# Three pairs of gate and up sums ahead of the first products: re-ordering the opening of a fused FFN-attention-FFN kernel on one core

## The reference

```
x = x + 0.5 * ffn(layernorm(x))
x = x + attn(layernorm(x))          # chunked gated linear attention, 4 heads
x = x + 0.5 * ffn(layernorm(x))

ffn(x): scores = softmax(x @ gate_w.T); keep the 8 best of 64, w_e
        flat = w_e[:, inv_map]                      # 8 groups of 8
        scalar = flat.sum(-1); soft = softmax(where(flat == 0, -1e9, flat))
        xg = x + soft @ mask_up_w                   # one per group
        g = xg @ gate_proj_w.T; u = xg @ up_proj_w.T    # 352 inner columns per group
        y = sum over groups of scalar * (silu(g) * u) @ down_proj_w.T
```

## Time and profile before

| | |
|---|---|
| median of 3 timed runs | 1857.75 us (1857.65 to 1857.84) |
| the profiled execution's own time | 1859.35 us |
| its span in the profile | 1857.6 us |
| TensorE busy | 1837.3 us (99%), 8608 matmuls |
| VectorE, ScalarE, GpSimd busy | 841.1, 525.6, 140.5 us (45%, 28%, 8%) |
| DMA | 366.83 MB, mean 197 GB/s |
| mean granted TensorE clock | 0.999 |

### The profile page before, as it was taken

One profiled execution on the slowest core, in us unless ns is written; L12 is line 12 of the kernel. 1 busy time (PEld: TensorE's weight loads), 2 busy tenths in 40 slices (PEclk: granted clock), 3 DMA queues, 4 the chain that ended last, 5 costly groups with the idle time before them and its releaser, 6 DMA issues.

```text
span 1857.6 us, 22348 instructions
## 1 busy us (share of the span) xinstructions
PE 1837.3 (99%) x8608; PEld 1529.7 (82%) x8608; DVE 841.1 (45%) x1599; ACT 525.6 (28%) x802; POOL 140.5 (8%) x246
## 2 busy tenths in 40 slices
PE   7999999999999999999999999999999999999999
PEld 5888888888888888888888888888888888888887
DVE  7557453555345563324433556344654324422222
ACT  3324322532124432112212533124532111311111
POOL 1131110100000000000010010000100000000000
PEclk9999999999999999999999999999999999999999
DMA  5986755445455455476655555455455466657664
GB/s 193 384 304 241 265 189 179 161 171 173 148 193 183 160 171 177 134 260 213 224 183 183 177 193 171 160 192 177 156 170 175 146 223 217 210 174 241 220 238 170
DMA packets 90345, 366.83 MB, mean 197 GB/s; under 512 B 11680, under 2 KB 12064, under 8 KB 69504
## 3 DMA queue, kind: packets, MB, share of 16 engines
q1 hardware_dynamic: 50064, 262.89, 40.3%
q10 hardware_dynamic: 27792, 47.20, 9.3%
q0 software_dynamic: 12384, 55.32, 7.7%
HBM read 323.55 MB, written 41.81 MB: 197 GB/s over the span
## 4 chain that ended last, share of the span: by engine, by line
PE 94%; DVE 3%; ACT 1%; issue 1%; DMA 0%; SPq 0%; ACTq 0%; DVEq 0%
PE bank L1057 27%; PE bank L1059 27%; PE bank L1058 27%; PE bank L1270 4%; PE bank L1067 1%; PE bank L1211 1%; PE bank L1203 1%; PE bank L1210 1%; PE bank L1197 1%; PE bank L1255 1%; PE bank L1256 0%; PE bank L1087 0%; PE bank L1088 0%; PE bank L1095 0%; DVE act_t L677 0%
## 5 line engine op out<-in xcount | busy, mean ns | idle before, releaser
L1057 PE MATMUL bank<-x_hi,wt 128*128 128x512 f32 x1328 | 524.0, 395 | 0.0
L1059 PE MATMUL bank<-x_lo,wt 128*128 128x512 f32 x1328 | 517.8, 390 | 0.0
L1058 PE MATMUL bank<-x_hi,wt 128*128 128x512 f32 x1328 | 517.0, 389 | 0.0
L677 DVE TENSOR_TENSOR act_t<-bank,sig 128x512 f32<-128x512 f32 x176 | 121.6, 691 | 568.9 <-PE bank L1270 511.7
L1059 PEld LDWEIGHTS bank<-x_lo,wt 128*128 128x128 f32 x1328 | 249.2, 188 | 53.2
L1058 PEld LDWEIGHTS bank<-x_hi,wt 128*128 128x128 f32 x1328 | 249.6, 188 | 50.2
L1057 PEld LDWEIGHTS bank<-x_hi,wt 128*128 128x128 f32 x1328 | 249.5, 188 | 49.5
L1057 PE MATMUL bank<-dt,a_hi 128*128 128x512 f32 x704 | 279.1, 396 | 0.3 <-DVE a_lo L677 0.3
L1059 PE MATMUL bank<-dt,a_hi 128*128 128x512 f32 x704 | 274.8, 390 | 0.0
L1058 PE MATMUL bank<-dt,a_lo 128*128 128x512 f32 x704 | 274.4, 390 | 0.0
L601 ACT ACTIVATE sig<-bank 128x512 f32<-128x512 f32 x176 | 105.5, 599 | 526.7 <-PE bank L1270 526.6
(11 more groups left out here) (178 smaller groups left out, 1684.0 us busy)
## 6 DMA issues: line engine op xcount, KB each, us to landing
wt<-scr_w SPq DMA_DIRECT2D x140, 1152.0 KB, 5.2
dt<-scr_d SPq DMA_DIRECT2D x140, 512.0 KB, 5.2
s_bc<-scr_s ACTq DMA_DIRECT2D x128, 256.0 KB, 5.1
state<-wat POOLq DMA_DIRECT2D x28, 512.0 KB, 6.4
scr_w<-wt POOLq DMA_DIRECT2D x12, 1024.0 KB, 7.9
b_all<-wgu SPq DMA_DIRECT2D x22, 512.0 KB, 7.9
scr_d<-dt POOLq DMA_DIRECT2D x22, 512.0 KB, 4.0
scr_w<-tw POOLq DMA_DIRECT2D x10, 1024.0 KB, 7.7
```

The costliest lines, as they stand in the source:

```text
L677: return nc.vector.tensor_tensor(dst, a, b, op)
L1057: mm(dst, wh, xh, start=start, stop=False)
L1058: mm(dst, wl, xh, start=False, stop=False)
L1059: return mm(dst, wh, xl, start=False, stop=stop)
```

## The change

GpSimd takes over the remainders of chunk 2 (`gu_lo(2)`), and ScalarE rounds chunk 2 ahead of five small DMA issues. Chunk 2's gate and up sums go to `YB[2]` and `YB[3]` and are computed before the `soft` products of chunk 0: the gate sums between the transposes of `scal` and `route`, the up sums behind those of `route`. The two transposed routing halves go to `W1` and `W0` instead. In the loop the gate sums of chunk 3 come with n = 2 and its up sums with n = 3, `masked(2)` and `masked(3)` stand in n = 1 and 2, and `down(0)`, `masked(4)`, `down(1)` come behind chunk 3's sums, `down(2)` and `down(3)` in n = 4. From n = 5 on the order is the old one. ScalarE's `m_top`, VectorE's `m_mask` and `m_rest` of chunks 3 and 4 move one chunk earlier, with n = 1 and n = 2; `gu_hi(4)` and `gu_lo(4)` stand in n = 2 ahead of the rest of it, and the decay weights move from n = 1 to n = 2.

```diff
         def g_bank(n):
-            return YB[0] if n == 1 else GB
+            return YB[2 * n - 2] if n in (1, 2) else GB
         def u_bank(n):
-            return YB[1] if n == 1 else UB
+            return YB[2 * n - 1] if n in (1, 2) else UB
...
+            def gu_lo(c):
+                pool.wait_ge(gu_hi_ok, c + 1)
+                w = first_w(c)
+                nc.gpsimd.tensor_tensor(w[:, GW:2 * GW], raw_gu[:, c % 2, :], w[:, 0:GW].bitcast(F32),
+                                        ALU.subtract).then_inc(gu_lo_ok, 1)
...
                 if c + 1 < CH:
                     store_w(c + 1)
+                if c == 0:
+                    gu_lo(2)
                 store_m(c)
...
             m_top(0)
+            gu_hi(2)
             act.dma_start(raw_k1, w_gk1).then_inc(ld_const, 16)
...
-            gu_hi(2)
             gu_hi(3)
...
                     silu(n)
+                    if n == 2:
+                        gu_hi(4)
                     pieces(3 * n)
                     pieces(3 * n + 1)
                     round_a(n)
-                    if n == 0:
-                        m_top(2)
-                    elif p == 0 and 1 < c < CH - 1:
+                    if n < 3:
+                        m_top(n + 2)
+                    elif p == 0 and 3 < c < CH - 1:
                         m_top(c + 1)
                     if n + 2 < PHASES * CH:
                         load_s(n + 2)
-                    if n == 1:
+                    if n == 2:
                         decay_weights()
                     if p == 0:
                         d_hi(c)
-                        if 0 < c < CH - 3:
+                        if 1 < c < CH - 3:
                             gu_hi(c + 3)
...
-            gu_lo(2)
+            dve.wait_ge(gu_lo_ok, 3)
             gu_lo(3)
...
                     gate(n)
-                    if n == 0:
-                        m_mask(2)
-                    elif p == 0 and 1 < c < CH - 1:
+                    if n < 2:
+                        m_mask(n + 2)
+                    elif n == 2:
+                        gu_lo(4)
+                    elif p == 0 and 3 < c < CH - 1:
                         m_mask(c + 1)
                     pieces(3 * n + 1)
                     rest_a(n)
-                    if n == 0:
-                        m_rest(2)
-                    elif p == 0 and 1 < c < CH - 1:
+                    if n == 2:
+                        m_mask(4)
+                    if n < 3:
+                        m_rest(n + 2)
+                    elif p == 0 and 3 < c < CH - 1:
                         m_rest(c + 1)
...
             router(0, 46)
+            pe.wait_ge(gu_lo_ok, 3)
+            main(g_bank(2), 0, 0, 2)
             router(0, 49)
             router(0, 50)
+            main(u_bank(2), P, 0, 2)
...
-                    if n > 1:
-                        pe.wait_ge(sig_ok, n if n > 2 else 1)
+                    if n == 2:
+                        loaded(0, 3)
+                        pe.wait_ge(sig_ok, 1)
+                        main(GB, 0, 0, 3)
+                    elif n > 3:
+                        pe.wait_ge(sig_ok, n)
                         main(GB, 0, p, c)
...
-                    if n > 1:
-                        pe.wait_ge(t1_ok, n if n > 2 else 1)
+                    if n > 2:
+                        pe.wait_ge(t1_ok, n if n > 3 else 1)
                         main(UB, P, p, c)
...
-                    if p == 0 and 1 < c < CH - 1:
+                    if n in (1, 2) or p == 0 and 3 < c < CH - 1:
                         masked(c + 1)
-                    if n == 2:
-                        pe.wait_ge(sig_ok, 2)
-                        pe.wait_ge(t1_ok, 2)
+                    if n == 3:
+                        pe.wait_ge(sig_ok, 3)
+                        pe.wait_ge(t1_ok, 3)
                         down(0)
-                    if n > 1:
+                        masked(4)
+                        down(1)
+                    elif n == 4:
+                        down(2)
+                        down(3)
+                    elif n > 4:
                         down(n - 1)
```

More of the change, by code:

```diff
@@ L152, in build, with soft_bank @@
         YB, GB, UB, W0, W1 = bank[0:4], bank[4], bank[5], bank[6], bank[7]
+        def soft_bank(p, i):
+            return W0 if p == 0 and i else W1
         def g_bank(n):
-            return YB[0] if n == 1 else GB
+            return YB[2 * n - 2] if n in (1, 2) else GB
         def u_bank(n):
-            return YB[1] if n == 1 else UB
+            return YB[2 * n - 1] if n in (1, 2) else UB
         def first_w(c):
@@ L496, in router @@
                         wait(act, u_ok, (p - 1) * CH)
-                    copy(softT[:, p % 2, i, :], (YB[i + 2] if p == 0 else W1)[:]).then_inc(route_cp, 1)
+                    copy(softT[:, p % 2, i, :], soft_bank(p, i)[:]).then_inc(route_cp, 1)
             def exps(t, pair):
@@ L1104, in router @@
                     pe.wait_ge(route_ok, p + 1)
[L1105 to L1110, removed]
+                    if i == 0:
+                        pe.wait_ge(scal_cp, p + 1)
+                    elif p:
+                        pe.wait_ge(route_cp, 2 * p + 1)
+                    else:
+                        pe.wait_ge(m_raw_ok, 2)
+                    b = soft_bank(p, i)
                     for j in range(NT):
@@ L1252, in masked @@
                 wait(pe, m_raw_ok, c)
+                if c == 2:
+                    pe.wait_ge(route_cp, 2)
                 hi, lo = weights(0, c)
@@ L1334, in _ @@
                     pieces(3 * n + 1)
-                    if p == 0 and 1 < c < CH - 1:
+                    if n in (1, 2) or p == 0 and 3 < c < CH - 1:
                         masked(c + 1)
-                    if n == 2:
-                        pe.wait_ge(sig_ok, 2)
-                        pe.wait_ge(t1_ok, 2)
+                    if n == 3:
+                        pe.wait_ge(sig_ok, 3)
+                        pe.wait_ge(t1_ok, 3)
                         down(0)
-                    if n > 1:
+                        masked(4)
[4 more added lines that the diff above has]
+                    elif n > 4:
                         down(n - 1)
                     pieces(3 * n + 2)
-                    if n == 1:
-                        masked(2)
             down(PHASES * CH - 1)
```

## The result

The changed kernel takes 1870.31 us (median of 4 runs, 1869.91 to 1871.52) against 1857.80 us (1857.65 to 1859.61) for the kernel before: a ratio of 1.0066, 95% interval 1.0049 to 1.0084. It is 12.5 us slower. On another occasion it took 1870.29 against 1859.62, a ratio of 1.0059 (1.0044 to 1.0074): the median of the changed kernel repeats, that of the one before wanders by 2 us. The profiled execution took 1870.22 us with a span of 1868.5, against 1859.35 and 1857.6: 10.9 us of difference by the profiles.

A forecast was written before the change was run, and what follows sets the result against it. TensorE, busy for 99% of the span, was taken as the bound. Terms -4.85 + 0.8 + 6.2 + 0.6 + 0.45 + 1.4 + 5.7 + 1.4 = +11.7 on 1857.75 gave 1869.5 us; 8-in-10 range 1862.5 to 1874.

The forecast's parts named there:

- The opening: PE from 32.95 to 40.99 us: chunk 2's sums cover the `route` and `softT` waits and keep the clock up; -4.85 us.
- Contention: GpSimd's subtraction for chunk 2 holds VectorE's `m_rest(0)` near 26 us and delays the router chain; +0.8 us.
- Stall A: PE waits in front of soft 3, 49.3 to 55.5 us, because `m_top(3)` waits for `store_m(1)`; 6.2 us.
- The landing: Time from issue of `store_m(1)` until it lands and frees `m_top(3)`; taken as 7.5 us, bounds 4.3 and 9.9.
- The estimate from the Trainium skill's figure: Rule of 2.0 us plus bytes over 436 GB/s, `store_d(0)` to `store_m(1)`: landing at 51.9, time near 1865.
- Stall B: PE waits in front of `down(0)` for gate(2), whose bank it overwrites; 0.6 us.
- slow soft products: Soft 3 runs at half rate after the 6 us idle; 0.45 us.
- Slow `down(0)`: `down(0)` runs its first 3 us at 1.2 GHz and takes 4.1 instead of 2.7 us; 1.4 us.
- Stall C: PE waits in front of chunk 4's gate sums for silu(3), queued behind `m_top(4)`, which needs `store_m(2)`; 5.7 us.
- The clock behind C: The granted clock falls again in the wait before chunk 4's gate sums; a further 1.4 us.
- Nothing given back: Later steps have cover and PE is the bound to the end, so the lost time stays lost.
- merely shifted: Sign against the forecast: it is wrong if the span beyond 75 us is not merely shifted.

The follow-up runs named there:

- s5: Kernel before with only the remainders of chunk 2 on GpSimd and ScalarE's rounding of chunk 2 ahead of the five DMA issues; 1859.94 us against 1859.62.
- s1: Changed kernel with mask stores of chunks 1 and 2 issued behind chunk 0's, those of 3 and 4 ahead of down stores 1 and 2; 1861.6 us.
- s7: Changed kernel with `store_m(1)` issued between `store_d(0)` and the 1 MB `store_w(2)` instead of behind both; 1868.11 us against 1870.29.
- s6: Changed kernel with 16 idle matmuls of 512 columns behind `down(1)`, into a bank nobody reads; 1869.09 us against 1870.29.
- s4: Kernel before with mask stores of chunks 1 and 2 behind chunk 0's, and chunk 3's ahead of down store 2; 1859.73 us against 1859.8.
- s2: Changed kernel with silu(3) behind `gu_hi(4)`, gate(3) behind `m_mask(4)` and decay weights in n = 6, stores unmoved; 1864.66 us against 1859.8 of before.

## Why the prediction was right, point by point

Forecast 1869.5, measured 1870.31. By the profile the forecast was +11.7 and the difference is 10.9. Gaps are taken here from start to start, one matmul of 512 columns counting 0.23 us; the listed waits are 0.15 us shorter, since they count from the shown end of the matmul ahead.

- *The opening gives 4.85.* It gave 4.76 (8.04 against 8.73 - 5.45). The covers held, and the clock stayed up (1.00 from 33 to 49 us).
- *Contention, +0.8.* 0.65 (`m_rest(0)` 1.07 for 0.42); s5 shows it alone. In the profile PE gets to the transposes of `scal` only 0.19 us later than before, because this execution's first steps happened to be 0.46 us earlier.
- *Stall A, 6.2.* 6.34 (48.78 to 55.12; listed as 6.18). The landing was 7.6 where I took 7.5. s1 shows the cause and s7 the dose. From `store_d(0)` to the landing of `store_m(1)` it is 45.47 to about 54.1, 8.7 us. The estimate from the Trainium skill's figure (DMA: Bandwidth & Descriptors, section Anatomy of one DMA), 5.9 us, is not borne out.
- *Stall B, 0.6, with 0.45 for slow soft products.* Together 1.07 (55.12 to 56.65 is 1.53 where two soft products take 0.46 at full rate), against 1.05.
- *Slow `down(0)`, 1.4.* 1.47: it took 4.20 us (56.65 to 60.85) where I had 4.1.
- *Stall C, 5.7.* 4.11 (64.56 to 68.67; listed as 3.96). This is the term that I mis-sized. `store_m(2)` landed 7.3 us after issue (I took 7.5), but from `m_top(4)` to the end of silu(3) were 3.84 us and not 5.25. I had taken 2.37 us for the two DMA issues of `load_s(4)`, from their 1.90 of the earlier trace rows; here they took 0.80, and the next rounding started 0.92 us behind `m_top(4)`. In s1 the same two took 1.88 and C was longer than I had said by as much. The DMA engines were busy in the two long cases (share 1.00 before, 1.04 in s1) and idle in the short one (0.00 from 64.69 to 65.49), but that does not explain it: at 70.96 of the changed kernel the two issues of `load_s(5)` took 0.92 us at a share of 0.99. Why they take 0.8 us or 1.9 stays open.
- *The clock behind C, 1.4.* 1.71 (7.16 for 5.45), and s6 shows that PE's idleness is its cause.
- *Nothing given back.* True, but the span behind 75 us is not merely shifted, which I had named as a sign of being wrong: there is a loss that I had not, 0.75 us near 340 us.

Sum of what was measured: -4.76 + 0.19 + 6.34 + 1.07 + 1.47 + 4.11 + 1.71 = 10.1 at chunk 5, where the side-by-side has 10.2; with the 0.75 it is 10.9, as by the spans. So no wait of this size is missing from the account. The forecast by the profile was 0.8 us too high, and that is what is left of errors of both signs: C was 1.6 us too long and the contention 0.6, against 0.3 of clock and 0.75 of the late step that I lacked. For the median of timed runs it came 0.8 us too low, because the kernel before took 1.6 us less in its timed runs than in its profiled one (12.5 us of difference by these medians, 10.7 in the second group). The three stalls and their causes were foreseen; that the total came within 1 us is in part luck.

**Left open.** The step near 340 us. There ScalarE waits for an attention slab:

```profile
334.01 1.06 ACT L432 ACTIVATE tw<-state 128x1024 fp32r<-128x1024 f32 x1 [2.57 <-DMA state<-wat]
```

The slab takes 8.0 us to landing, 6.6 before, with loads of the same kinds beside it. The wait was 1.2 us before and PE lost nothing; here silu comes late behind it and PE waits 0.5 us at 343.59. The step shows in every kernel with the new order and not in s4 or s5. I don't know why the slab lands later, and tried nothing on it.

## What to carry to other kernels

When work is brought forward, follow each buffer that its last wait needs back to the DMA that frees it, and then ask what stands ahead of that DMA in its queue. A wait that the profile shows as harmless (1.5 us on ScalarE before) is a wait whose cover you may be about to move. Small stores that free a buffer belong ahead of large ones that free nothing soon: here that order cost nothing in the old kernel and gave back 8.7 us of the new one.

## What the runs showed of the hardware

The granted clock can fall after the idleness is over. In stall C PE stood from 64.7 to 68.67 at a granted clock of 1.00; it fell near 69.7, when four matmuls of the next sums had run at full rate, and stayed at 0.50 until about 73. A stall of 3.3 us (s1) cost the same 1.7 us, and none was paid where idle matmuls filled the stall (s6, 5.46 us for the same sums).

A pair of DMA issues on ScalarE took between 0.80 and 1.90 us in these runs, and everything behind it on ScalarE moves with that. It took 1.90 in the kernel before (54.18) and 1.88 in s1 (54.62), with the DMA engines full (shares of 1.00 and 1.04), and 0.80 in the changed kernel with them idle (64.69). But 0.92 at a share of 0.99 (70.96 of the changed kernel) and 1.15 at 0.07 (62.79 of s2) say that the load at that moment does not set it.

In each of the three cases seen, an instruction of VectorE with two SBUF inputs that ran beside GpSimd's two-input instruction ended only behind it, by 0.27 to 0.56 us (in s5 it took 1.06 us instead of 0.42). The MAX8 instructions of one input beside it were not held (0.61 us for four in s5).
